# Cross attentions 0 and 1: score units and value products in four blocks a step in place of eight

## The reference, cut to what matters

```python
x = x + _L0_xattn_ref(_layernorm(x, axis=-1), ctx_1024, mask_BxS2_ik0, ...)
    # q, k, v = projections of x and of the context, split into 16 heads
    scores = q @ k.T * scale          # 256 queries x 4096 keys, per batch and head
    scores = scores + ext             # masked keys get a huge negative number
    attn = softmax(scores)            # needs the row maximum before exp
    out = attn @ v
```

## Time and profile before

| | us |
|---|---|
| three runs | 2007.07, 2013.03, 2017.22 |
| median | 2013.03 |
| the profiled execution | 2011.96 |
| its span, first to last instruction | 2010.7 |
| cross attention 0, first to last unit | 66.8 to 486 |
| cross attention 1, first to last unit | 706 to 1123 |

### The profile page before, as it was taken

The page is one execution under the profiler, slowest core; times in us unless marked ns, Lnnn a source line. Parts: engine busy times, 40 slices in busy tenths (PEclk is TensorE's granted clock), DMA queues, the critical chain, the costliest instruction groups (busy, mean ns, idle before and its releaser), DMA issues.

```text
span 2010.7 us, 37964 instructions
## 1 busy us (share of the span) xinstructions
PE 1888.7 (94%) x14112; PEld 1198.1 (60%) x14134; DVE 1365.7 (68%) x3210; ACT 1251.5 (62%) x2818; POOL 624.5 (31%) x737
## 2 busy tenths in 40 slices
PE   7999999999999899999999889999988799899999
PEld 4555555554465455555555457789556688565656
DVE  3776668785668587666789377654276898578382
ACT  3687778897354378777888563376264786265251
POOL 2111111112641211111110175585052466355151
PEclk9999999999999999999999999999999899999999
DMA  9777668762101777667764204153202332200110
GB/s 210 160 147 137 115 117 164 128 111 91 42 22 47 113 149 149 135 114 138 150 106 76 87 2 145 48 173 105 68 2 77 93 116 64 89 2 9 42 56 11
DMA packets 114358, 191.55 MB, mean 95 GB/s; under 512 B 17224, under 2 KB 67200, under 8 KB 107648
## 3 DMA queue, kind: packets, MB, share of 16 engines
q1 hardware_dynamic: 113184, 188.11, 42.8%
q10 hardware_dynamic: 992, 1.02, 0.3%
HBM read 135.20 MB, written 2.69 MB: 69 GB/s over the span
## 4 chain that ended last, share of the span: by engine, by line
PE 65%; DVE 22%; ACT 7%; issue 3%; DMA 2%; POOL 1%; SPq 0%; DVEq 0%; POOLq 0%; ACTq 0%
DVE WK L881 10%; PE PS L818 8%; PE PS L704 8%; PE PS L721 5%; PE PS L372 5%; PE PS L380 5%; PE PS L692 4%; PE PS L733 4%; PE PS L2427 2%; PE PS L2369 2%; PE PS L529 2%; PE PS L481 2%; ACT WK L580 2%; PE PS L508 2%; PE PS L1299 1%
## 5 line engine op out<-in xcount | busy, mean ns | idle before, releaser
L881 DVE TENSOR_REDUCE WK<-PS 128x1 f32<-128x1024 f32 x512 | 621.6, 1223 | 219.1 <-PE PS L704 163.0
L989 ACT ACTIVATE WK<-PS 128x512 f32<-128x512 f32 x840 | 464.4, 601 | 37.2 <-PE PS L704 22.7
L704 PEld LDWEIGHTS PS<-QSR,KSR 51*128 51x128 f32 x2048 | 249.0, 185 | 243.1 <-ACT WK L989 91.2
L704 PE MATMUL PS<-QSR,KSR 51*128 51x256 f32 x2048 | 376.2, 305 | 10.9 <-ACT WK L989 1.8
L692 PE MATMUL PS<-KSR,QSR 51*128 51x512 f32 x1024 | 366.1, 446 | 7.1 <-DMA KSR<-scratch_mask 2.6
L818 PE MATMUL PS<-WK 128*32 128x256 f32 x2528 | 218.1, 392 | 0.5 <-ACT WK L973 0.5
L1012 POOL TENSOR_TENSOR WK<-WK 128x512 fp32r<-128x512 f32 x62 | 79.3, 1278 | 431.9 <-ACT WK L950 220.5
L692 PEld LDWEIGHTS PS<-KSR,QSR 51*128 51x128 f32 x1024 | 183.8, 184 | 16.8 <-issue 9.9
L580 ACT ACTIVATE WK<-PS,WK 128x256 f32<-128x256 f32 (+1 forms) x320 | 140.4, 450 | 71.1 <-DVE WK L548 42.0
L1065 POOL TENSOR_SCALAR nbw<-WK 128x4 fp32r<-128x4 f32 x64 | 12.6, 197 | 353.3 <-DVE WK L887 346.0
L610 POOL TENSOR_TENSOR WK<-WK 128x512 f32<-128x512 f32 x96 | 99.8, 1039 | 55.4 <-DVE WK L563 37.7
(11 more groups left out here) (373 smaller groups left out, 3803.9 us busy)
## 6 DMA issues: line engine op xcount, KB each, us to landing
KSR<-WK SPq DMA_DIRECT2D x381, 128.0 KB
WB<-in_ctxT SPq DMA_DIRECT2D x78, 512.0 KB, 5.1
WK<-in_ctxT SPq DMA_DIRECT2D x40, 512.0 KB, 4.1
WK<-in_ctx SPq DMA_DIRECT2D x32, 512.0 KB, 3.9
WA<-in_ctxT SPq DMA_DIRECT2D x26, 512.0 KB, 5.2
QSR<-scratch_q SPq DMA_DIRECT2D x48, 128.0 KB, 4.3
WB<-in_L3f_qkv SPq DMA_DIRECT2D x2, 1536.0 KB, 6.4
WB<-in_L3f_w SPq DMA_DIRECT2D x2, 1536.0 KB, 9.6
```

The costliest lines, as they stand in the source:

```text
L704: return pe.e.matmul(tile["S", L, s, i][:, j * 256:j * 256 + 256], KS[s % 4][HALF[i % 2], kt * 128:(kt + 1) * 128], QS[HALF[i % 2], g % 2, ...
L881: dv.e.tensor_reduce(mt[:, n:n + 1], tile["R", L, s, n].rearrange("p a b -> p (a b)"), AX, ALU.max).then_inc(*dv.at("R", L, s, n))
L989: ac.e.activation(PR[n % NPR], tile["S", L, s, i], ACT.Exp).then_inc(*ac.at("E", L, s, i))
```

## The change

The loop over eight units becomes one over four blocks of two units. In a block both units come first and then two rounds: rounds 2b-2 and 2b-1 behind blocks 1 and 2; the last two or three rounds of the step before behind block 0; round 4 behind block 3, followed by the bias transposes and the key tile (or, from step 24 on, round 5). The value tile stands behind the rounds of block 1. ACT's copy of the bias rows stands behind all of unit 6. In units 12 and 13 of the list, "S" no longer stands ahead of "U". Nothing is computed otherwise, and the rings stay as they are. Line numbers of the changed kernel are one less.

```diff
-        for u in range(8):
-            n = (u + 4) % 8
-            r = s + (1 if u < 4 else 2)
-            row = (r, n) if r < 32 else None
-            if u == 6:
-                yield "S", s, 12
-                yield "MC", s + 1
-                yield "U", s, 12, row
-                yield "U", s, 13, row
-                yield "S", s, 13
-            else:
+        for b in range(4):
+            for u in (2 * b, 2 * b + 1):
+                n = (u + 4) % 8
+                r = s + (1 if u < 4 else 2)
+                row = (r, n) if r < 32 else None
                 for i in (2 * u, 2 * u + 1):
                     yield "U", s, i, row
                     yield "S", s, i
-            if row:
-                yield "R", r, n
-            if u == 1 and 0 < s < 23:
-                yield "L", s + 1
-            if u < 2 and s:
-                yield "F", s - 1, 5 if u == 0 and s < 25 else u + 6, u + 7
-            if u == 1 and s:
-                yield "E0", s - 1
-            if u == 2 and 8 <= s < 16:
-                yield "V", 1, s - 8, s
-            elif u == 7 and s < 24:
-                yield "K", s // 4 + 2, s % 4
-            elif u >= 2:
                 if u == 6:
-                    yield "M", s + 1
-                yield "F", s, u - 3 if u == 3 and 8 <= s < 16 else u - 2, u - 1
+                    yield "MC", s + 1
+                if row:
+                    yield "R", r, n
+                if u == 1 and 0 < s < 23:
+                    yield "L", s + 1
+            if b == 0:
+                if s:
+                    yield "F", s - 1, 5 if s < 25 else 6, 8
+                    yield "E0", s - 1
+            elif b == 3:
+                yield "F", s, 4, 5
+                yield "M", s + 1
+                if s < 24:
+                    yield "K", s // 4 + 2, s % 4
+                else:
+                    yield "F", s, 5, 6
+            else:
+                yield "F", s, 2 * b - 2, 2 * b
+                if b == 1 and 8 <= s < 16:
+                    yield "V", 1, s - 8, s
```

## The result

| | before | after |
|---|---|---|
| median of the runs, us | 2015.12 (4 runs) | 2101.37 (4 runs) |
| ratio, 95% interval | | 1.0435 (1.0414 to 1.0457) |
| the profiled execution, us | 2011.96 | 2099.58 |

A forecast was written before the change was run, and what follows sets the result against it. PE, busy 94% of the span, paces plain units without gaps, and what counts is who waits for whom. Step terms sum to 51.1 us per attention, 102.2 for two, on a 2013.03 median: 2115 us, range 2085 to 2140.

The forecast's parts named there:

- the side with 0.93: The forecast's sign for the whole kernel: slower, given a chance of 0.93.
- Part 1: Plain blocks: one change each way between units and rounds in place of two, saving 0.3 to 0.35 us of 2.47.
- Part 2: Plain blocks: the odd unit's second half waits for a score bank; 2.64 us against 2.47, +0.17.
- Part 3: After the key tile: unit 1 waits for ACT's eviction; unit 0 to 2 takes 3.79 us against 2.92, +0.87.
- Part 4: Before the key tile: it waits for unit 7's maximum; unit 6 to next unit 0 takes 5.13 against 4.67, +0.46.
- Part 5: Steps with key and value tile: the value tile's eviction is uncovered between units 4 and 6; +2.13 us a step.
- Part 6: Late steps +0.98 us; step 24 +1.32; steps 30 and 31 estimated at +1.6 and +1.2; step 0 +0.9.
- Soft gate: Rival: ACT returns the first bank early enough for blocks to run at DVE's 2.45; 2079 us, chance 0.08.
- Heavier: Rival: PE's longer waits lower the granted clock to the 1.2 GHz level; about 2160 us, chance 0.07.
- Faster: Rival: the saved drains between units and rounds decide, row tiles come 0.3 to 0.4 us earlier a step; 1988, chance 0.05.

The follow-up runs named there:

- s4_after_both: The changed kernel with exponentials over 64 columns only and row maxima over every second key; measured 1990.83 us.
- e3_end_start: The changed kernel with block 0 and the end of a step both put back as before; measured 1.0112 times the kernel before.
- s5_before_both: The kernel before with exponentials over 64 columns only and row maxima over every second key; measured 1977.36 us.
- s3_after_max: The changed kernel with row maxima over every second key only, exponentials at full length; measured 2081.09 us.

## Why the prediction was right

The forecast was +102 us on 2013, measured +86 (2015.12 to 2101.37), in the range and on the side with 0.93. By its own steps:

*Part 1, fewer changes.* 0.3 to 0.35 a block was forecast (its own terms, 0.20 to 0.23 and 0.14, add up to 0.34 to 0.37). With quick exponentials and maxima 0.23 shows (s4_after_both), and the bank's return may still hold a little there: the last half starts 0.05 after the exponential that frees its bank. The trace of the full kernel cannot show it, and the sum did not use this term by itself.

*Part 2, the score banks.* 2.64 forecast, 2.62 to 2.63 measured in the plain blocks (except in steps 26 and 27 of attention 0, where ACT also sums weights), and 2.42 with the exponential at 0.38. This term was the surest, because each of its five addends is a row.

*Part 3, after the key tile.* 3.79 forecast for unit 0 to 2, 3.79 measured in attention 0. In attention 1 it is 3.61, because there the eviction is a plain copy, 0.60 and 0.59 us in place of 0.69 and 0.68 with the bias, and unit 1 starts 1.35 after unit 0, not 1.53. I took a row of attention 0 for both: this mis-sized the term by 0.17 in 24 steps, 4 us. Three rounds take 1.43 from 370.36 to 371.79, as put together from one and two.

*Part 4, before the key tile.* 5.13 forecast, 5.04 measured. The term that was mis-sized is "two maxima of 1.22": one after the other they take 2.35, not 2.44. The lag of 0.06 and the 1.87 held. 0.09 in 46 steps, 4 us.

*Part 5, the value tile.* +2.13 forecast, +2.07 and +1.92 measured; 6.27 and 3.17 against 6.15 to 6.3 and 3.17.

*Part 6, late and odd steps.* Late steps +0.98 forecast, +0.91 in attention 1. In attention 0 the steps that also sum weights hid part of it (+0.66 on average). Steps 30 and 31 were estimates: step 30 lost 2.0 (1.6 forecast). Step 31 goes from 10.66 to 11.85 from its first unit to its last round, +1.2 as forecast, but no row stood behind that number, so the hit is luck in part. Step 0 of attention 1 became 0.6 shorter, 0.9 longer was forecast. Most of this gap is the clock's and not the order's: in the kernel before the granted clock was 0.50 from 709.4 to 712.8 us, inside that step (706.3 to 720.1), and in the changed kernel it was 1.00 all through. Of the kernels with full exponentials and maxima, the one other whose clock fell there (e3_end_start) has the step at 14.2 and the kernel before at 14.0; those without the fall have it at 13.0 to 13.4. What the order itself does to that step stays open.

Added up over the steps, the attentions grew by 47.1 and 43.4 us from their first unit to their last round in the profiled executions, 90.5 together; the stretches outside them became 3 us shorter, which the forecast had at nothing. The sum for the attentions was 102.2, 11.7 too much: about 4 from the eviction, 4 from the maxima, 2 from the late steps, 1.5 from step 0 of attention 1, and small things that partly cancel. The mechanisms of the waits stood; sizes were off, and all the larger errors lie on the same side.

*The rivals.* Soft gate: excluded by blocks of 2.63. Heavier: the clock was 1.00 in both attentions. Faster: its condition, unit 1 within about 1.0 of unit 0, is not met (1.53 and 1.35), and s4_after_both shows that even with quick exponentials and maxima the wait for the eviction outweighs the saved changes in steps with a key tile of attention 0 and equals them in attention 1.

## What to carry to other kernels

Grouping alike matmuls saves PE time, here 0.23 us a group, only if the ring of banks is deep enough for the longer group: the time from the first tile's matmul to its bank's return (0.55+0.60+0.06) has to be under what PE does before it needs that bank again. Work of another kind between two groups is often the cover of somebody's eviction; before it is moved, write down which eviction lies under it. In this case such a change could be costed from rows to a few tenths of a microsecond a step, where every row was taken from the very stage and layer that it stands for.

## What the runs showed of the hardware

Two maxima of 128x1024 fp32 from PSUM in a row take 2.35 us (363.73 above), so the second starts 1.13 to 1.14 after the first, as 191 pairs of the changed kernel do, while a single one is 1.22 long. The profiled lengths overlap. (The prediction called DVE nearly full in a plain unit, at 1.22 a maximum.) A row of maxima at a pitch of 1.24, as the old order has, was therefore set by PE, and DVE had more slack than the 1.22 suggests; with maxima of 0.69 (s5_before_both) the units kept their pitch.

The granted clock fell to 0.50 at places that differ between these kernels: for 3.4 us inside step 0 of attention 1 in the kernel before, and for 17.1 us at the end of attention 1 in s3_after_max, where a block of 2.62 took 4.07. A step that looks longer or shorter than its like should be read with the clock of its own stretch beside it.

The profile names a releaser "ACT" for many loads of weights before units with 0.41 us idle. The same 0.41 stands there in s4_after_both, where the exponentials are over long before, with no releaser ("issue"), so it is no wait for ACT. A wait may show on the row of the matmul itself (0.23 before 372.99, 0.78 before 369.53), but it need not: the second half of unit 5 in step 19 starts at 375.61, 0.05 behind the exponential that it needs, and has idle time (0.28) on its load of weights alone. What tells a wait is the end of the instruction that is waited for, not the idle time.
